# Self-attention in chunks of 512 rows beside its own steps, with K laid out block-diagonally by transfers

## The reference

```python
x = x + xattn(ctx, ctx, layernorm(x), lens, lens, Wk, bk, Wq, bq, Wv, bv)   # 64 queries on 1601 context rows
x = x + attn(layernorm(x), W_w, W_b, proj_w, proj_b, ln_g, ln_b, rpb)       # 64 rows on themselves
x = x + ffn(layernorm(x), w_gate, w_up, w_down)                              # quantised, 256 -> 768 -> 256

def attn(x, ...):
    q, k, v = split(x @ W_w.T + W_b)                # 16 heads of 16
    a = q @ k.T / sqrt(256); a = where(causal, -inf, a) + bias(rpb)
    out = softmax(a) @ v @ proj_w.T + proj_b
    y = x + out
    return (y - mean(y)) / sqrt(var(y) + 1e-5) * ln_g + ln_b

def ffn(x, ...):                                    # act_qdq: scale by the maximum of the whole tensor
    x = act_qdq(x)
    up, gate = act_qdq(x @ dq(w_up).T), act_qdq(x @ dq(w_gate).T)
    o = act_qdq(act_qdq(gate * fixed_qdq(sigmoid(gate))) * up)
    return o @ dq(w_down).T
```

## Time and profile before

| | |
|---|---|
| median of 3 runs | 1679.34 us (1678.31 to 1681.15) |
| the profiled execution, its own time | 1679.94 us |
| its span, first to last instruction | 1678.0 us |
| TensorE busy | 1451.8 us, 87% |
| VectorE busy | 1111.4 us, 66% |
| ScalarE busy | 893.9 us, 53% |
| GpSimd busy | 856.2 us, 51% |
| granted TensorE clock, mean | 0.934 |

### The profile page before, as it was taken

The page is one execution under the profiler, slowest core; times in us unless marked ns, Lnnn a source line. Parts: engine busy times, 40 slices in busy tenths (PEclk is TensorE's granted clock), DMA queues, the critical chain, the costliest instruction groups (busy, mean ns, idle before and its releaser), DMA issues. The chain is left out here.

```text
span 1678.0 us, 55602 instructions
## 1 busy us (share of the span) xinstructions
PE 1451.8 (87%) x24345; PEld 1019.8 (61%) x24345; DVE 1111.4 (66%) x1735; ACT 893.9 (53%) x1188; POOL 856.2 (51%) x567
## 2 busy tenths in 40 slices
PE   4789999999999999999999999999958388358608
PEld 2356777776777776777776677777644377333206
DVE  7756666666666666666666666666635599685984
ACT  1446665556566555666555566656543144434752
POOL 5567666556666555666655566655305355621000
PEclk9899999999999999999999999999988588768858
DMA  5553354443345444345444334444213300010001
GB/s 169 127 140 101 104 128 117 115 140 101 101 114 129 111 125 125 101 105 128 115 118 138 101 101 113 124 114 111 62 53 75 77 1 0 1 57 0 0 0 51
DMA packets 84295, 154.93 MB, mean 92 GB/s; under 512 B 15376, under 2 KB 47896, under 8 KB 84064
## 3 DMA queue, kind: packets, MB, share of 16 engines
q1 hardware_dynamic: 82704, 150.52, 34.5%
q10 hardware_dynamic: 1360, 0.98, 0.2%
HBM read 61.08 MB, written 2.20 MB: 38 GB/s over the span
## 5 line engine op out<-in xcount | busy, mean ns | idle before, releaser
L638 DVE TENSOR_REDUCE MXP<-W_PS 128x1 f32<-128x512 f32 x768 | 499.1, 687 | 284.8 <-PE W_PS L450 284.8
L534 ACT ACTIVATE PR<-S_PS 128x1024 f32<-128x1024 f32 (+1 forms) x416 | 424.6, 1022 | 260.2 <-PE S_PS L398 252.2
L344 POOL TENSOR_TENSOR K_HI<-K,MCOL 128x512 f16<-128x512 f32 (+1 forms) x224 | 219.0, 978 | 427.2 <-ACT K L542 426.0
L346 POOL TENSOR_TENSOR K_LO<-K,K_HI 128x512 f16<-128x512 f32 (+1 forms) x224 | 291.9, 1303 | 17.6
L450 PE MATMUL W_PS<-STK,QS 105*128 105x512 f16 (+1 forms) x1024 | 269.8, 335 | 9.0 <-POOL STK L371 4.8
L398 PE MATMUL S_PS<-QS,STK 105*128 105x128 f16 (+1 forms) x3328 | 256.1, 220 | 1.0 <-DVE QS L652 1.0
L413 PEld LDWEIGHTS O_PS<-PR,V 128*17 128x17 f32 x13312 | 190.8, 97 | 80.0 <-issue 59.9
L413 PE MATMUL O_PS<-PR,V 128*17 128x64 f32 x13312 | 231.4, 220 | 8.4 <-ACT PR L534 7.4
L433 PE MATMUL W_PS<-WV_HI,CTX_HI 128*128 128x256 f16 (+1 forms) x832 | 228.3, 274 | 1.6 <-DVE WV_LO L611 1.4
L398 PEld LDWEIGHTS S_PS<-QS,STK 105*128 105x128 f16 (+1 forms) x3328 | 201.4, 99 | 44.8 <-DVE QS L652 1.1
L433 PE MATMUL W_PS<-WV_HI,CTX_LO 128*128 128x256 f16 (+1 forms) x832 | 227.8, 274 | 0.0
(11 more groups left out here) (219 smaller groups left out, 1720.6 us busy)
## 6 DMA issues: line engine op xcount, KB each, us to landing
CTX<-in_ctx_t SPq DMA_DIRECT2D x64, 800.5 KB, 5.9
STK<-K_HI SPq DMA_DIRECT2D x256, 128.0 KB, 2.5
STK<-K_HI SPq DMA_DIRECT2D x256, 72.1 KB, 2.1
STK<-K_LO SPq DMA_DIRECT2D x128, 128.0 KB, 2.6
STK<-K_LO SPq DMA_DIRECT2D x128, 72.1 KB, 2.1
QSTK<-STK SPq DMA_DIRECT2D x12, 192.0 KB
SK<-QK_HI SPq DMA_DIRECT2D x8, 256.0 KB, 5.2
SQS<-QK_HI SPq DMA_DIRECT2D x8, 256.0 KB, 5.0
```

The source lines that it names most:

```text
L344: pool.tensor_tensor(K_HI[:, m, lo:hi], k32, zero, ALU.add).then_inc(k_hi, 1)
L346: pool.tensor_tensor(K_LO[:, m, lo:hi], k32, K_HI[:, m, lo:hi], ALU.subtract).then_inc(k_lo, 1)
L534: nc.scalar.activation(PR[0:m, par, :], S_PS[par][0:m, :], ACT.Exp).then_inc(p_sb, 1)
L638: dve.tensor_reduce(MXP[:, j, at:at + 1], bank[:, :], AX.X, ALU.max).then_inc(mx_done, 1)
```

## The change

Three things move.

1. The setup is cut by chunks of 512 rows (four tiles). `SETUP` makes the first chunk's Q, K and V ahead of step 0. `BESIDE` makes the other three beside steps 0 to 11: in `body` the units stand behind the projection on TensorE, behind exp on ScalarE, behind the normalising on GpSimd, and on VectorE ahead of the row sums of s-1. All steps are unrolled.
2. Q is no longer spread by products on VectorE. Instead, K's tensor `KZ` is zeroed once (two halves, on GpSimd), and SP fills it block-diagonally: 24 transfers of 16 partitions for each chunk, beside 12 of 32 partitions for Q (`SQS`). The scores are then 32 matmuls with 64 stationary columns.
3. Work of the end moves ahead. The projection's bias goes in as a row of `WP`. The scales are made in three groups (`NORMS`) by a guess and three Newton steps on VectorE, the output's LayerNorm runs from step 13 on (`ADDED`), the feed-forward's own LayerNorm, its transposes and maxima stand in the steps 16 to 18 and behind them, and its gate weight is read, scaled and turned in the setup.

VectorE's list in a step also has another order: scores plus bias and maximum of s, projection of s-3, setup units, row sums of s-1. `S_PS` is single, `T` triple.

The core of the diff:

```diff
-        for dst, m0, parts in ((SK, 2, (QK_HI, QK_LO, QK_HI)), (SQS, 0, (QK_HI, QK_HI, QK_LO))):
-            ...
-                    sp.dma_start(dst[32 * q:32 * q + 32, c::4, :], part[32 * c:32 * c + 32, m0:m0 + 2, :])
+        for r in range(TILES // 4):
+            u = r % 2
+            sp.wait_ge(sm["qk_lo"], 4 * r + 2)
+            if r >= 2:
+                sp.wait_ge(sm["s_ps"], 4 * (r - 1))
+            for c in range(4):
+                for q, part in enumerate((QK_HI, QK_HI, QK_LO)):
+                    sp.dma_start(SQS[32 * q:32 * q + 32, u, c::4, :], part[32 * c:32 * c + 32, u, 0:2, :]).then_inc(stacked[r], 16)
+            sp.wait_ge(sm["qk_lo"], 4 * r + 4)
+            ...
+            for c in range(4):
+                for q, part in enumerate((QK_HI, QK_LO, QK_HI)):
+                    for a in range(2):
+                        lo = 32 * q + DH * a
+                        sp.dma_start(KZ[lo:lo + DH, u, c::4, a, :], part[32 * c + DH * a:32 * c + DH * a + DH, u, 2:4, :])

+SETUP = [
+    ("TN", 0, 0), ("TN", 0, 1), ("QK", 0, 0), ("QK", 0, 1), ("QK", 0, 2), ("QK", 0, 3), ("VV", 0, 0), ("VV", 0, 1),
+    ("WT", 0, 0), ("WT", 0, 1), ("WT", 0, 2), ("WT", 0, 3),
+]
+BESIDE = {
+    **{4 * r - 4: [("TN", r, 0), ("TN", r, 1), ("QK", r, 0)] for r in range(1, 4)},
+    **{4 * r - 3: [("QK", r, 1), ("QK", r, 2)] for r in range(1, 4)},
+    **{4 * r - 2: [("QK", r, 3), ("VV", r, 0)] for r in range(1, 4)},
+    **{4 * r - 1: [("VV", r, 1)] for r in range(1, 4)},
+    16: [("XT", 0, 0), ("XT", 0, 1)], 17: [("XT", 1, 0), ("XT", 1, 1), ("XT", 2, 0)],
+}

 GpSimd, ahead of the steps
+        pool.memset(KZ[:, 0]...); pool.wait_ge(sm["in_small"], 16 * N_SMALL); affine_select of BIAS, twice
+        pool.wait_ge(sm["wg_max"], 3)
+        pool.tensor_tensor(blk, blk, wide[0], ALU.mult).then_inc(sm["wg_int"], 1)
+        pool.memset(KZ[:, 1]...)
+        for x in SETUP[:6]:
+            setup(x)                               # QK_LO of chunk 0
+        pool.wait_ge(sm["wg_clip"], 2)
+        pool.tensor_tensor(blk, blk, wide[1], ALU.mult).then_inc(sm["wg_val"], 1)

 TensorE, step s
+                need(pe, sm["t_a"], s)
+                for j in range(PAIRS):
+                    for w in range(2):
+                        cols = slice(lo + w * SQ, lo + (w + 1) * SQ)
+                        for a in range(2):
+                            last = pe.matmul(S_PS[SQ * a:SQ * (a + 1), (2 * j + w) * SQ:(2 * j + w + 1) * SQ],
+                                             SQS[0:96, r % 2, j, cols], KZ[0:96, r % 2, j, a, cols], ...)
+            ...                                    # PV of s-2, projection of s-3
+            for x in BESIDE.get(s, []):
+                setup(x)
+            if live(s - 1):
+                pe.wait_ge(sm["t_norm"], t + 1)    # then eight transposes of T

 VectorE, step s
+            if live(s):
+                dve.wait_ge(sm["s_ps"], s + 1)
+                dve.tensor_tensor(T[:, s % 3], S_PS..., BIAS..., ALU.add).then_inc(sm["t_a"], 1)
+                dve.tensor_reduce(MX[:, s % 2], T[:, s % 3], AX.X, ALU.max).then_inc(sm["t_max"], 1)
+            if live(s - 3):
+                dve.wait_ge(sm["y_ps"], t + 1)
+                dve.tensor_tensor(XN[:, t, :], Y_PS[:, 0:D], XN[:, t, :], ALU.add).then_inc(sm["y_sb"], 1)
+                dve.bn_stats(STAT[:, t, :], XN[:, t, :]).then_inc(sm["y_stat"], 1)
+            for x in BESIDE.get(s, []):
+                setup(x)
+            if s == 13:
+                scale_rows(*NORMS[0], 0)
+            add_rows(ADDED.get(s, ()))
+            if live(s - 1):
+                dve.wait_ge(sm["t_exp"], t + 1)
+                dve.tensor_reduce(SM[:, t % 2], T[:, t % 3], AX.X, ALU.add).then_inc(sm["t_sum"], 1)
+                dve.reciprocal(SM[:, t % 2], SM[:, t % 2]).then_inc(sm["t_sum"], 1)
+            if s == 16:
+                ...                                # scales and sums of tiles 0 to 13, first maximum
```

More of the change, by code:

```diff
@@ L891, in _ @@
+        for r in range(TILES // 4):
+            sp.wait_ge(stacked[r], 16 * PARTS)
     @block.tensor
     def _(pe):
-        for t in range(TILES):
-            pe.wait_ge(sm["xn2"], t + 1)
-            if t % 2 == 0 and t >= 4:
-                pe.wait_ge(sm["tr_lo"], t // 2 - 1)
-            for k in range(KT):
-                last = pe.transpose(RINGS[t // 2 % 2][:, (2 * k + t % 2) * P:(2 * k + t % 2 + 1) * P],
-                                    XN[:, t, k * P:(k + 1) * P], CST[:, C_ID:C_ID + P])
-            last.then_inc(sm["tr_ps"], 1)
@@ L937, in body @@
+        for x in SETUP:
+            setup(x)
+        for s in range(STEPS):
+            if live(s):
+                r, lo = s // 4, s % 4 * P
+                if s % 4 == 0:
+                    pe.wait_ge(stacked[r], 16 * PARTS)
+                need(pe, sm["t_a"], s)
                 for j in range(PAIRS):
                     for w in range(2):
-                        last = pe.matmul(S_PS[u][:, (2 * j + w) * SQ:(2 * j + w + 1) * SQ],
-                                         QZ[:, u, j, w, :, :],
-                                         SK[:, j, bass.ds(s * P + w * SQ, SQ)], start=True, stop=True, skip_group_check=True)
@@ L1019, in _ @@
-        for i in range(TILES):
-            nc.scalar.activation(XN[:, i, :], XN[:, i, :], ACT.Identity, bias=VT[:, i:i + 1], scale=RS[:, i:i + 1])\
-                .then_inc(sm["y_normal"], 1)
+                nc.scalar.activation(T[:, s % 3], T[:, s % 3], ACT.Exp, scale=1 / 16).then_inc(sm["t_exp"], 1)
+            if s == 16:
+                act.wait_ge(sm["chain"], CHAIN * 2)
+                normal_again(range(0, 4))
+            if s == 17:
+                normal_again(range(4, 10))
+            for x in BESIDE.get(s, []):
+                setup(x)
@@ L1023, in _, with setup @@
+        act.wait_ge(sm["chain"], CHAIN * 4)
+        normal_again(range(10, 14))
+        setup(ENDING[0])
+        setup(ENDING[1])
+        act.wait_ge(sm["chain"], CHAIN * 6)
+        normal_again(range(14, 16))
+        setup(ENDING[2])
     @block.gpsimd
     def _(pool):
+        def setup(x):
+            kind, r, i = x
+            if kind == "QK":
+                n, m = number[x] + 1, qk_rows(i)
+                pool.wait_ge(sm["qk_32"], n)
+                pool.tensor_tensor(QK_LO[:, r % 2, m, :], QK32[:, (n - 1) % 3, :], QK_HI[:, r % 2, m, :], ALU.subtract)\
+                    .then_inc(sm["qk_lo"], 1)
@@ new lines, in normal @@
+        def normal(tiles):
+            for t in tiles:
+                dve.tensor_scalar(XN[:, t, :], X[:, t, :], MV[:, t, 0:1], RS[:, t:t + 1], ALU.subtract, ALU.mult).then_inc(sm["xn"], 1)
+        deviations(dve, STAT, MV, VE[:, :], SD[:, :], RS[:, :], VT[:, :], sm["ln2"], sm["root2"])
+        normal(range(0, 4))
+        normal(range(4, 8))
+        setup(SETUP[0])
+        setup(SETUP[1])
+        dve.wait_ge(sm["w_hi"], 1)
+        dve.scalar_tensor_tensor(WLO[:, :, :], WRAW[:, :, :], W_SCALE, WHI[:, :, :], ALU.mult, ALU.subtract).then_inc(sm["w_lo"], 1)
@@ L1163 @@
+        maximum(1)
+        dve.wait_ge(sm["y_stat"], 16 + 14)
+        scale_rows(*NORMS[2], 4)
+        add_rows(range(*NORMS[2]))
+        dve.wait_ge(sm["y_stat"], 16 + 16)
+        scale_rows(*NORMS[2], 5)
+        for i in range(2, len(MAXIMA)):
+            maximum(i)
+        dve.wait_ge(sm["xm"], len(MAXIMA))
+TURN = {8: 0, 16: 1}
 GATE_SCALED = 2
```

678 lines of the change are left out of this document (348 added, 330 removed).

## The result

The changed kernel takes **1749.87 us** (median of 4 runs, 1746.98 to 1752.68) against 1680.03 for the kernel before beside it: a ratio of 1.0417, 95% interval 1.0397 to 1.0436. The profiled execution has a span of 1748.5 us and a time of its own of 1750.19; its mean granted clock is 0.919.

A forecast was written before the change was run, and what follows sets the result against it. VectorE never rests in 7.3 us steps before; afterwards a closed chain through its late row sums bounds them. 1679.9 - 20 (setup) + 98.2 (steps) - 14.3 (end) - 2.6 (feed-forward) = 1741, +14 (clock): 1755 us, range 1705 to 1780.

The forecast's parts named there:

- Time of the first scores: Setup: GpSimd's late QK_LO, then 36 SP issues at 0.64 us, put first scores at 1297 against 1317, 20 us saved.
- The closed lap: Self-attention steps: scores, VectorE's step, row sums, normalising, transposes, next scores form one chain, 9.9 us against 7.3; chance 0.72.
- The rival that the busiest engine sets the step: Steps: chain not closed, TensorE sets 7.6 us with chunk work and 5.4 without, total 1640; chance 0.08.
- The rival that the transfers back up (1825): Chunks: queue backs up at 1.28 us an issue, first scores +23, three waits +15.6 each; chance 0.06.
- The scores' price: TensorE, each step: 32 score matmuls of half the weight columns taken at 1.28 us, bounds 0.64 and 1.28.
- The plain step: Step without setup work: 9.9 us at the full clock against 7.3 before, 4.2 longer at 1.2 GHz.
- the clock term: TensorE idles 4.5 us a plain step and slows: 4.2 us for three and a bit of four last steps, +14.
- Chunk steps: Steps with setup work, 0 to 11: 13.6, 9.9, 12.3 and 11.0 us, four together 46.8; chunk 0's steps 44.
- Waits for K: Scores of steps 4, 8, 12 wait for K's 24 transfers: 6.6 us, in the last chunk 2.2 more.
- Steps 12 to 15 and the clock: Last four steps: 9.9, 17.2 and two of 13.95 us, 55.0 in all with LayerNorm work, plus 14 for the clock.
- The rival that the clock stays low throughout, 1808: All sixteen steps: TensorE at the low clock, 4.2 us more each on 1741; chance 0.12.
- End and feed-forward: After the steps: 43.2 us to the first low part, -14.3; up weight's reduction earlier in the feed-forward, -2.6.

The follow-up runs named there:

- Experiment 11: Changed kernel with each of GpSimd's two zero fills of the K buffer written as eight short fills: 1748.05 us, one run.
- Experiment 5: Changed kernel with GpSimd making chunk 0's four QK_LO before the gate weight scaling and second zero fill in the setup: 1741.82 us, ratio 1.0387.
- experiment 1: Kernel before the change, with only VectorE's row sums and reciprocal of s-1 moved from the head of a step to its end: 1773.10 us, ratio 1.0556.
- experiment 2: Changed kernel with VectorE's row sums of s-1 first in a step and GpSimd normalising s-1 before subtracting for s: 1704.86 us, ratio 1.0155.
- experiment 6: Changed kernel with 12 of K's 24 transfers a chunk left out, so the output is not the reference's: 1725.30 us, ratio 1.0283.
- Experiment 7: Changed kernel with extra unread matmuls filling TensorE's gaps in steps 12 to 15: 1746.15 us, ratio 1.0404.
- experiment 8: Changed kernel with row sums, normalising and low parts first, K's units before Q's, and ScalarE issuing eight Q transfers a chunk: 1677.70 us, ratio 0.9999.

## Why the prediction was right, step by step

The forecast was 1755, the result 1749.87, by the mechanism that was named. The profiled execution (1750.19) is 4.9 under the forecast, and that is a sum with both signs in it: steps -6.0, end +2.2, feed-forward -1.1. The -6.0 is itself +7.7 in the chunk steps, -6.8 in the waits for K and -6.9 in the last four steps, so it is in part luck that the total came this near.

**Time of the first scores: 1297 forecast, 1297.07 measured, partly by luck.** The issues are as taken (0.63 to 0.64 each, landing 2.0 us): the first went at 1272.35, 24.7 us ahead of the scores, forecast 1271.7 and 25.1. But the cross-attention ended 2.5 us earlier in this execution than in that of before. Counted from there the setup is 17.4 us shorter, not 20. Two things come in that I had not priced: the zero fill kept VectorE from a 0.18 us operation for 2.1 us, and the four QK_LO took 6.1 us, the first two of them 3.6 and not 2.3, beside VectorE's scaling of the gate weight. GpSimd's timeline:

```profile
1268.64 6.08 POOL L1151 TENSOR_TENSOR QK_LO<-QK,QK_HI 128x512 f16<-128x512 f32 x4
```

Experiment 11 shows that the first of them is not simply won back: the first scores came no earlier with it gone. Experiment 5 confirms that GpSimd's order sets this time. The pieces are of 64 KB (Q) and 32 KB (K), not of 32 and 16 as I wrote for the setup; it made no difference to the issue.

**The closed lap: right, and shown from both sides.** Making it in the kernel before costs 94 us (experiment 1), undoing it in the changed one gives 45 (experiment 2), though the waits for K take 21 of what it frees. The rival that the busiest engine sets the step is out: VectorE is busy for 53% of the four last steps, and less in the others; TensorE for at most 66%. The rival that the transfers back up (1825) is out as well: the issues stay at 0.64 us but for a few.

**The scores' price: mis-sized.** I took 1.28 us for the 32 matmuls of half the weight columns because the moving columns are the same. They take 0.69 at the high clock and 1.06 at the low, against 0.64 and 1.01 for the 16 of full width: my other bound was the right one, 0.6 us a step. By the Trainium skill, TensorE: Matmul & The Clock Gate, "Part 3: Packing small matmuls", small matmuls on different columns of the array run beside one another; the rows agree with that, as the two halves of each pair go to different partitions of S_PS, but they can't tell it from a price by weight columns.

**The plain step.** 9.9 forecast at the high clock, 14.1 with the clock term; 12.07 measured in step 12. By its legs: to the projection 5.85 (4.36 and 7.7 were taken at the two clocks; PV was slow, the projection partly), the row sums' and GpSimd's legs as taken, transposes 1.90 (the low clock's price). Step 5, at a clock of 0.79 on average over the chunk, takes 9.6.

**Chunk steps.** Without waits the three groups of four take 45.6, 49.1 and 50.6 us, forecast 44, 46.8 and 46.8. The 7.7 us more are mostly the low clock, which I charged to steps 12 to 15 only, and the scores' 0.6 us a step too much hides part of it. The granted clock reads 0.70, 0.79 and 0.77 there. The excess stands in steps 6, 7, 10 and 11, which take 1.6 to 1.7 us more than my 12.3 and 11.0, and in step 9 (11.1 against 9.9); chunk 0 has 1.6 more. In step 7 PV takes 1.91 us and the transposes 1.97, against 1.09 and 1.04 at the high clock. That step of the prediction ("in steps 0 to 11 QK and VV fill part of that") gave the units too much credit.

**Waits for K.** Forecast 6.6, 6.6, 8.8; measured 4.85, 3.97, 6.34, in all 6.8 less. The mechanism was right (experiment 6 removes all three), and the cover was larger: steps 3, 7 and 11 without their waits last 12.1 to 12.6 us, not 11.0.

**Steps 12 to 15 and the clock.** 55.0 forecast and +14 for the clock; measured 62.1, 7 above the 55.0. By its rows the low clock cost these steps 9.9 us: scores 1.5 in all, PV 2.9, projection 1.8 (in two of them it ran at the high clock), transposes 3.7. My plain sum had 2.4 too much in it for the scores, and 55.0 - 2.4 + 9.9 is 62.5. So the 14 was mis-sized because I took the projection at the low clock each time and the scores at twice 1.01; the four terms that it is made of also add up to 4.4 us a step, not 4.2. Experiment 7 fits: its rows have 4.7 us less of the low clock, and it was 3.9 faster there. And I read the clock of before too kindly: I wrote 0.65 in one stretch of 8 us and full in others, but the others of its loop (1348 to 1428) read between 0.79 and 1.00. One of them, from the kernel before:

```profile
1388.00:1396.00 8.00, 6.54 (x93) 5.22 (x92) 7.74 (x11) 3.23 (x5) 4.59 (x3) 0.79 0.00 0
```

Sixteen steps: 222.6 us; 228.6 were forecast with the clock.

The rival that the clock stays low throughout, 1808, is out: the granted clock is 0.66 to 0.79 in the four stretches, between the levels. In steps 6, 7, 10 and 11 the transposes stand behind 4.2 us of waiting and take 1.97 us each time; in steps 4, 5, 8 and 9 they stand behind 1.8 us and take 1.09. The rule that was weighed (the Trainium skill, TensorE: Matmul & The Clock Gate, section "HAM oscillation — how this bites in real kernels"), that a TensorE idle between bursts falls to the low clock each time, is borne out here behind the longer waits and not behind the shorter ones. Experiment 7 shows that work in the gap raises the clock, and that this gave about 1 us a step over the four steps, since a lap holds other engines' legs that no clock of TensorE changes.

**End and feed-forward.** From the end of step 15 (1519.67) to the first low part (1565.11) 45.4, forecast 43.2; from there on 183.4 against 187.1 before, -3.7 where -2.6 was forecast. The forecast's own terms, 8.7 less three chunks of 1.85, make 3.1 there and not 2.6.

## What to carry over

In a loop pipelined over tiles, write down one lap of waits with each engine's order in it before counting what each engine has to do: moving one 1.5 us operation behind a wait cost 94 us here, with no engine given anything more to do; some of that was TensorE's clock, which fell in the gaps that the order opened. When a lap is shortened, ask at once what ran in its shadow: 36 DMA issues at 0.64 us a chunk from one queue were hidden but for 4 to 6 us, and each speed-up of the steps laid more of them bare until they were started earlier and shared with a second queue. And a setup is as long as the most loaded in-order queue in it; here that was GpSimd, and putting its four urgent operations first gave 8 us with nothing else changed.

## What the runs showed of the hardware that I had not expected

**GpSimd and VectorE exclude each other in some operations.** Beside a zero fill of 3.51 us a VectorE operation of 0.18 us took 2.30 and one of 0.96 took 4.23; both end with the fill or within 0.9 us of its end. The aggregation that ran beside the same fill was not held (1.17 us, as in the earlier trace rows). The kernel before had it too, and I had not read it: the two QZ products took 2.52 us, with GpSimd's subtraction beside them from 1365.82 to 1367.89, and 0.87 in experiment 1, where GpSimd was idle at that time. So of the 2.5 us that the change took from VectorE, 1.65 were waiting. The Trainium skill, SBUF — State Buffer, section "SBUF: two separate sides", has this rule: the two share a pair of ports that is locked for a whole instruction, and the loser is blocked. The trace agrees, with the numbers above.

**DMA issues cost the queue about the same for any small piece.** 0.60 to 0.64 us each for 32 and 64 KB within SBUF from SP, but for a few longer ones (four in 3.34 us once), and 8 in 5.35 us from ScalarE (0.67), during which ScalarE started nothing else in experiment 8.
